# Input stage and attention in one block: no barrier between them, hand-placed SBUF, first operands loaded inside the input stage

## The reference

```python
def attn(x, w_attn, w_proj, adapter, gating):     # B=2, T=1024, C=512, 32 heads of 16
    q, k, v = split(x @ w_attn.T)                 # then rotary embedding on q and k
    attn = softmax(causal(q @ k.T / 4))
    y = attn @ v
    y = y + gating * softmax(q @ ak.T / sqrt(C)) @ av   # ak, av from 10 adapter rows
    return y @ w_proj.T

x = x + layernorm(attn(layernorm(x)))
x = x + layernorm(ffn(layernorm(x)))              # silu(x Wg.T) * (x Wu.T) @ Wd.T, F=1376
```

## Time and profile before

| | before |
|---|---|
| time, median of 3 runs | 1303.68 us (1301.52 to 1308.1) |
| the profiled execution's own time | 1300.54 us |
| span of the profile, first to last instruction | 1298.6 us |
| PE, DVE, ACT, POOL busy in the span | 88%, 56%, 39%, 21% |
| mean granted clock of PE | 0.928 |

### The profile page before, as it was taken

The page is one execution under the profiler, slowest core; times in us unless marked ns, Lnnn a source line. Parts: engine busy times, 40 slices in busy tenths (PEclk is TensorE's granted clock), DMA queues, the critical chain, the costliest instruction groups (busy, mean ns, idle before and its releaser), DMA issues. The chain is left out here.

```text
span 1298.6 us, 18975 instructions
## 1 busy us (share of the span) xinstructions
PE 1142.8 (88%) x7036; PEld 773.0 (60%) x7036; DVE 721.0 (56%) x968; ACT 507.5 (39%) x1058; POOL 269.3 (21%) x261
## 2 busy tenths in 40 slices
PE   3999998389999999999999994883999999999996
PEld 1777887145445444444444433662787787887785
DVE  4756755376777777777777513894223423324323
ACT  3133223025666666666666652441111111111111
POOL 1524524701111111111111111663000100001001
PEclk9999999558999999999999966886999999999998
DMA  7346346862444443434430005882100200200200
GB/s 259 97 112 171 112 115 180 160 105 50 77 84 89 85 77 76 75 75 75 76 75 19 18 25 177 254 284 81 65 1 1 97 1 2 98 1 17 81 1 33
DMA packets 82515, 113.01 MB, mean 87 GB/s; under 512 B 24964, under 2 KB 42500, under 8 KB 82436
## 3 DMA queue, kind: packets, MB, share of 16 engines
q1 hardware_dynamic: 82436, 111.92, 34.2%
HBM read 68.83 MB, written 42.21 MB: 86 GB/s over the span
## 5 line engine op out<-in xcount | busy, mean ns | idle before, releaser
L700 ACT ACTIVATE prob<-ps_s 128x512 f32<-128x512 f32 (+3 forms) x768 | 314.9, 505 | 190.1 <-PE ps_s L811 181.5
L723 DVE TENSOR_REDUCE neg<-ps_m 128x2 f32<-128x1024 f32 (+2 forms) x224 | 248.8, 1147 | 108.7 <-PE ps_m L781 73.8
L811 PE MATMUL ps_s<-q_op,k_op 50*128 50x512 f32 (+2 forms) x768 | 264.2, 449 | 29.0 <-ACT prob L700 26.0
L776 PE MATMUL ps_m<-k_op,q_op 48*128 48x512 f32 (+2 forms) x768 | 200.9, 428 | 34.4 <-DMA vg<-v_groups 23.0
L811 PEld LDWEIGHTS ps_s<-q_op,k_op 50*128 50x128 f32 x768 | 122.7, 192 | 158.7 <-ACT prob L700 93.8
L678 POOL TENSOR_SCALAR_AFFINE_SELECT prob<-prob 128x512 f32<-128x512 f32 x128 | 81.6, 637 | 445.1 <-ACT prob L700 445.1
L825 PE MATMUL ps_y<-prob,vg 128*17 128x512 f32 (+3 forms) x1536 | 155.6, 525 | 0.6 <-POOL prob L678 0.6
L1216 DVE TENSOR_TENSOR hf<-sl,ps_u 128x512 f32<-128x512 f32 (+1 forms) x44 | 30.2, 687 | 189.4 <-PE ps_u L72 189.4
L776 PEld LDWEIGHTS ps_m<-k_op,q_op 48*128 48x128 f32 x768 | 103.4, 199 | 51.4 <-issue 23.7
L723 DVE TENSOR_REDUCE neg_far<-ps_m 128x4 f32<-128x512 f32 (+2 forms) x96 | 97.6, 1045 | 37.9 <-PE ps_m L781 37.9
L1285 PE MATMUL ps_d<-w_ffn_high,wp_high 128*128 128x512 f32 (+1 forms) x352 | 115.6, 391 | 0.0
(11 more groups left out here) (161 smaller groups left out, 1769.2 us busy)
## 6 DMA issues: line engine op xcount, KB each, us to landing
raw<-in_w_ffn SPq DMA_DIRECT2D x16, 520.0 KB, 5.5
k_op<-k_parts SPq DMA_DIRECT2D x32, 256.0 KB, 5.1
q_op<-q_parts SPq DMA_DIRECT2D x64, 128.0 KB, 6.0
y_heads<-y_sb SPq DMA_DIRECT2D x32, 256.0 KB, 5.0
v_groups<-v_out SPq DMA_DIRECT2D x16, 272.0 KB, 3.9
vg<-v_groups SPq DMA_DIRECT2D x16, 272.0 KB, 6.9
x<-in_x SPq DMA_DIRECT2D x4, 1024.0 KB, 12.8
q_parts<-part_h SPq DMA_DIRECT2D x16, 256.0 KB, 2.9
```

Of the source, the lines that this page charges most:

```text
L700: act.activation(prob[:, v % NPROB, h, unit_cols(u)], ps_s[:, y % NS, unit_cols(u)], ACT.Exp, scale=D ** -0.5).then_inc(s_exp, 1)
L723: nc.vector.tensor_reduce(to[:, :, pairs[0]:pairs[-1] + 1, i - TT * c], scores, axis=AX.X, op=ALU.max, negate=True).then_inc(a_read, 1)
L776: last = nc.tensor.matmul(ps_m[:, g % 2, s, base:base + wide], q_op[buf][r, c, pair, (i - TT * c) * P:(i - TT * c + 1) * P], k_op[buf][r, ...
L811: nc.tensor.matmul(ps_s[:, y % NS, lo:BLK], k_op[buf][r, pair, j * P:(j + 1) * P], q_op[buf][r, c, pair, lo:BLK], start=True, stop=True)\
```

## The change

The two stages become one block. There is no barrier between them: each engine goes on from its last instruction of the input stage to its first of attention, and waits there only for the semaphores that guard the memory it takes over (`inputs_done`). SBUF is laid out by hand (`Map`): `k_op0`, `q_op0`, all `vg` and the masks have room of their own, the other three operand buffers lie over `x`, `wqk_h` and `wqk_l`. `x` has two buffers in place of four, so blocks 2 and 3 of x are loaded later. The loop over b is unrolled. Masks and the ones of `k_op0` are built by POOL before the first block, the ones of `k_op1` before block 3. ACT issues the loads of groups 0 and 1 itself, in blocks 2 and 3, right behind high_of(1). PE goes through 10 entries before the first unit in place of 27, and group 0's units carry the rest: after its four c = 0 units everything up to (0, "turn", 1) has been issued. `heads` and `wp_high` move before group 1, `wp_low` before group 2's first mask. `wp_raw` is loaded behind maxima(0, 1). The statistics and normalization that each block makes for the next are dropped in block 3, where they were not used.

```diff
+def load_group(engine, d, operands, op_in, n):
+    q_op, k_op, vg = operands
+    ...
+    for s in range(2):
+        r = 64 * s
+        engine.dma_start(k_op[buf][r:r + 2 * D].bitcast(F32), k[n, s]).then_inc(op_in[buf], 16)
+        engine.dma_start(k_op[buf][r + 2 * D:r + 3 * D].bitcast(F32), k[n, s, 0:D]).then_inc(op_in[buf], 16)
+        for c in range(HB):
+            engine.dma_start(q_op[buf][r + D:r + 3 * D, c].bitcast(F32), q[n, s, c]).then_inc(op_in[buf], 16)
+            engine.dma_start(q_op[buf][r:r + D, c].bitcast(F32), q[n, s, c, 0:D]).then_inc(op_in[buf], 16)
+    engine.dma_start(vg[buf][:], d["v_groups"][n]).then_inc(op_in[buf], 16)
...
         rstd_of(0)
+        build_masks(pool, passed, ident_h, causal_h, mask_const)
+        ones_below(pool, passed, k_op[0], op_const[0])
...
+                    if b == 1 and step == (high_of, 1):
+                        act.wait_ge(op_const[half], 2)
+                        for s in range(2):
+                            act.wait_ge(parts_out[s], 16 * 4 * 2 * HB)
+                            act.wait_ge(v_stored[s], 16 * 2 * HB)
+                        load_group(act, d, operands, op_in, half)
...
-    first_main = at[(1, EARLY)]
+    first_main = at[(0, "turn", 0)] + 1
...
-        if u == p == 0:
+        if p == 0 and u == 0 or n == p == 0 and u == TT:
             goal = at.get((n + 2, EARLY), len(order))
-            rate = sum(read_time(e) for e in order[todo:goal]) / sum(spot_time[i:i + NU * 2])
+            end = i + (NU - u) * 2
+            if n == u == 0:
+                goal, end = at[(0, "turn", 1)] + 1, i + TT * 2
+            rate = sum(read_time(e) for e in order[todo:goal]) / sum(spot_time[i:end])
...
+        maxima(0, 0)
+        load(2)
+        maxima(0, 1)
+        inputs_done(sp, "xn", "ya")
+        sp.dma_start(wp_raw[:], d["wp"]).then_inc(wp_in, 16)
...
+        pe.wait_ge(mask_in, 32)
+        inputs_done(pe, "rope")
         for g in range(first_main):
             for_maxima(g)
+        inputs_done(pe, "v_out", "pT", "ya_out")
```

More of the change, by code:

```diff
@@ L562, in stage_attention @@
             todo += 1
[L563 removed]
+        if i + 1 == end:
             beside[n, u, p] += range(todo, goal)
             todo = goal
[L567 to L850 removed]
@@ new lines, in _ @@
+    @block.gpsimd
+    def _(pool):
+        inputs_done(pool, "qk")
+        wait_alone(pool, passed, done["low"][0][1], done["low"][1])
+        for buf in range(2, NBUF):
+            ones_below(pool, passed, k_op[buf], op_const[buf])
+        inputs_done(pool, "parts")
+        for rows in (32, 64):
+            pool.memset(inv[rows:rows + 32], 0.0).then_inc(inv_const, 1)
+        wait_alone(pool, passed, inv_const, 2)
+        for n in range(NG):
+            if n == 2:
+                inputs_done(pool, "rot")
+                pool.wait_ge(wp_high, 1)
+                pool.tensor_tensor(wp_l[:], wp_raw[:], wp_h[:].bitcast(F32), op=ALU.subtract)
+            for u, (c, j) in enumerate(units):
+                if j < TT * c:
+                    continue
+                pool.wait_ge(s_exp, HG * (NU * n + u + 1))
+                diag = prob[:, (NU * n + u) % NPROB, :, (j - TT * c) * P:(j - TT * c + 1) * P]
+                pool.affine_select(out=diag, in_=diag, compare_op=ALU.is_ge, fill=0.0, base=0,
+                                   pattern=[[0, HG], [1, P]], channel_multiplier=-1).then_inc(masked, 1)
@@ new lines, in _, with take_y @@
+    @block.scalar
+    def _(act):
+        def take_y(n, c):
+            act.wait_ge(pv, NU * n + units.index((c, TT * (c + 1) - 1)) + 1)
+            if n:
+                act.wait_ge(y_out[c], 16 * n)
+            act.activation(y_sb[:, c], ps_y[:], ACT.Copy).then_inc(y_ready, 1)
+        inputs_done(act, "high", "low", "scores", "v")
+        for n in range(NG):
+            if n == 1:
+                inputs_done(act, "ya", "rot")
+                act.activation(heads[:].rearrange("p (h w) -> p h w", w=D), over(ident[0:KR, 0:H], D, 2), ACT.Copy)
+                act.wait_ge(wp_in, 16)
+                act.activation(wp_h[:], wp_raw[:], ACT.Copy).then_inc(wp_high, 1)
+            for u in range(NU):
+                v = NU * n + u
+                if v >= NPROB:
+                    act.wait_ge(pv, v - NPROB + 1)
+                for h in range(HG):
+                    y = HG * v + h
+                    act.wait_ge(s_ps, y + 1)
+                    act.activation(prob[:, v % NPROB, h, unit_cols(u)], ps_s[:, y % NS, unit_cols(u)], ACT.Exp,
+                                   scale=D ** -0.5).then_inc(s_exp, 1)
+                if u == 0 and n:
+                    take_y(n - 1, 1)
+                if u == TT:
+                    take_y(n, 0)
+        take_y(NG - 1, 1)
```

1242 lines of the change are left out of this document (617 added, 625 removed).

## The result

| | before | after |
|---|---|---|
| median | 1301.51 us (20 runs, 1289.35 to 1327.12) | 1305.34 us (20 runs, 1301.79 to 1313.72) |
| ratio after / before | | 1.0059, 95% interval 1.0032 to 1.0086 |
| the profiled execution: time, span, mean granted clock | 1300.54, 1298.6 us, 0.928 | 1311.89, 1310.2 us, 0.916 |

A forecast was written before the change was run, and what follows sets the result against it. It took the handoff's 22.98 us PE gap and the half-clock ramp as the loss; group 1's first scores 14.4 us earlier, less 3.0 later, gave 11.4 us net and 1292.3 us against the median 1303.68, range 1278 to 1303.

The forecast's parts named there:

- The gap: PE's idling at the handoff from input stage to attention: all 22.98 us were to go.
- C: Rival: in blocks 2 and 3 late stores and dearer ACT issues take most of the gain; 1300 us, chance 0.20.
- X: The time of group 1's first scores: forecast at 299.6 us, 14.4 us earlier than before.
- s: The end of the input stage's last adapter product on PE: 223.0 us before, forecast at 229.8.
- masks in the input stage: POOL's masks and ones run beside DVE's first normalization and delay the stage by 0.7 us.
- ACT's issues and the transfers, blocks 2 and 3: ACT's 13 issues delay PE 2.0 us a block, 4.1 in all; later-landing stores add 2 us.
- units with c = 0: Group 0's first units, carrying 15 entries where before 7, at DVE's price: 18 us.
- second row wait: Before group 0's first scores with c = 1, PE waits for the second turn's rows: 4.8 us.
- units with c = 1: Group 0's later units with 24 entries, the clock rising midway: 31 us, between 26 and 38.
- later costs: Behind group 1's first scores: heads and wp_high make PE wait 2.5 us, wp_low costs 0.5 us.
- D: Rival: in blocks 2 and 3 ACT waits for stores behind the loads, 12 us a block; 1314 us, chance 0.10.
- rival B: Behind the handoff PE's clock stays up or returns at once; net gain 17.4, 1286 us, chance 0.20.

The follow-up runs named there:

- e3: e1 plus 13 DMAs of 16 bytes a row, into a tile nobody reads, issued by ACT behind high_of(1); ratio to before 1.0036.
- e1: Changed kernel with the loads issued by SP at the start of blocks 2 and 3, none by ACT; ratio to before 0.9962.
- e2: Changed kernel with ACT's loads moved to the start of blocks 2 and 3, ahead of high_of(0); ratio to before 0.9884.
- e6: e5 with both groups' loads issued by SP behind its last stores, still without the barrier; ratio to before 1.0103.
- e4: Changed kernel with attention's list of entries as in the kernel before, loads still on ACT behind high_of(1); ratio to before 0.9996.
- e5: Changed kernel with the edits of e2 and e4 together; 1286.65 us, ratio to before 0.9894.
- e10: Changed kernel with wp_raw loaded ahead of the first rows, and heads and wp_high ahead of the first exponential; ratio to before 1.0006.
- e11: e9 with a needless 1.9 us copy on ACT at the start of the sixth group; ratio to before 0.9948.
- e7: e5 with a matmul that nobody reads behind entries of the ramp, about 20 of them; ratio to before 0.9989.
- e9: e5 with wp_raw loaded ahead of the first rows, and heads and wp_high ahead of the first exponential; 1281.1 us, ratio to before 0.9853.
- e8: Changed kernel with ACT's loads one step later, behind exp_of(0); ratio to before 1.0126.

## Why the prediction was wrong

The gap went as forecast, and so did the kind of the waits. Their sizes didn't, and no rival described the result: C came nearest in number (1300), but by a mechanism that didn't occur. X was read from the row at 314.02. The same row now stands at 308.69, where 299.6 was forecast. (By counting, the group's first scores stand 0.65 us ahead of that row, in both kernels.) The terms (s was forecast as 229.8 and is 234.8):

| term | forecast | measured |
|---|---|---|
| masks in the input stage | +0.7 | -1.1 (end of block 1) |
| ACT's issues and the transfers, blocks 2 and 3 | 4.1 + 2 | 12.8 |
| s to group 0's first scores (11.5 + 4.5) | 16.0 | 14.8 |
| units with c = 0 | 18 | 19.2 |
| second row wait | 4.8 | 4.7 |
| units with c = 1 | 31 | 35.2 |
| second group longer than before ("later costs") | 3.0 | 7.9 |

1. **ACT's 13 issues: the step that failed.** I took 13 issues at 0.47 us, 6.1 us in all, the exponential 2.0 us late by it, and carried that 2.0 through to PE. The issues took 8.3, which my upper price of 0.64 us had (8.3 us exactly). But what was queued behind them wasn't only late: it fell onto the start of POOL's `part_l`, and `a_prob` grew from 0.49 to 2.51 us. In the order of before it began 1.2 us ahead of `part_l` and was through. I had named the steps behind the issues and priced them as if they slid without changing. So the 2.0 us a block were mis-sized in two steps: the exponential was 4.5 us late in place of 2.0, and the delay grew by another 2.0 on its way to PE. e3 shows that issues without bytes suffice for most of it, even where they took 6.3 us; e1 and e2 show that without issues at that place most of the loss is gone. What is left of the 12.8 is the share of the unrolled stage and the transfers: e6, with no load in the stage, takes 1.5 us more than before for blocks 2 and 3, and kernels with early loads at the block's start 0 to 3.5 on top. The Trainium skill (SBUF — State Buffer, SBUF: two separate sides) says that a VectorE operation with two SBUF inputs and a GpSimd one that reads SBUF take the shared port pair in turn, and the one that starts second is fully blocked. By that rule `a_prob`, begun at 158.16, ends only after `part_l` (160.33); the trace agrees, it ended at 160.67.
2. **The transfers: rivals C and D fell.** Stores in blocks 2 and 3 landed in 3.1 to 5.3 us in the median of each kind (before, in block 2, 2.9 to 4.0, the `v_out` stores 4.0), not in 8 to 14, and e3 loses most of it without bytes. The trace agrees with the rule of the Trainium skill that the prediction quotes (transfers of all issuing engines interleave): SP's stores landed in these times beside ACT's loads. The same section of the Trainium skill calls the issue time usually small relative to the DMA. Here an issue took 0.31 to 1.44 us and its load landed after 5.0 to 7.2. That is small, and no comfort: on ACT, among steps that PE waits for, it was most of the cost.
3. **The ramp: the forecast was near, the comparison missing.** The row waits were sized about right (5.43 and 4.74 against 4.5 and 4.8). What I never asked was what the handoff would give with the old list, under which 17 entries cover the wait. e4 and e5 show it: 7 to 8 us better (e4 against after, e5 against e2). So of the 10.2 us of the two row waits the earlier units earned back only some 3. The units with c = 1 were mis-sized as well: 35.2 us and not 31, near the 38 of a half clock throughout. The clock was at half for 20 of these 35 us.
4. **Later costs and the clock.** I priced `heads` and `wp_high` at their own 2.5 us. The wait came (2.15 us), but from it on the clock was at half for 20 of 24 us, and the group took 7.9 us more than before to the mark of group 2. This is a second step that failed: the wait was priced at its own length. e10, that one edit, gives 9.5 us in that group; e11 makes the same loss again at a place of my choosing. Against rival B the clock did fall, as forecast, in the ramp. The prediction quotes the Trainium skill for the rule that activity releases the slow clock. e7 agrees with it: at 0.50 in 225:235, with the additions 1.00 from 235 us on. A PE busy for 9.85 of 10 us at 0.50 (e5, 265 to 275 us) remains, as the earlier trace rows, a stretch where the slow clock is not released at once.

Added up at group 3 (after less before, 2.6 us): the gap gives 23.0; blocks 2 and 3 take 12.8, less 1.1 from block 1; the row waits take 10.2 and the second group 7.9 more. These make +6.8; the rest of group 0's entries and units, which ran partly at full clock, give 4.2 back. The forecast was a gain of 11.4, so it missed by 14.0. Up to rounding these are 6.7 in blocks 2 and 3, 4.9 in the later costs, 4.2 in the units with c = 1, 1.2 in those with c = 0, less 1.8 in the term of the masks and 1.3 up to group 0's first scores and in the second row wait.

**What stays open.** Why the clock falls in some groups of some executions with no wait over 0.32 us in sight (after's 540 to 557, e9's 305 to 315). In after, e1, e5 and e8 such a fall begins some 7 us behind a group's first scores and costs 10 us in two groups; the same stretch passes without a fall in most other groups. Why block 1 ends 1.1 us earlier. And whether `a_prob` alone could have been saved, by another order on POOL, wasn't tried.

## What to carry to other kernels

DMA issues on a compute engine are instructions of that engine: put them where its next consumer has slack, which the trace shows as its idle time, and check what each delayed step will newly run beside. A wait on the critical engine must be priced with the clock that it may lose; 2 us cost 8 to 10 here, so work that holds a feeding engine belongs where that engine is idle, not where it is merely free on average. When a change removes a gap and reorders the work behind it, cost the two apart: the old order behind the new handoff was the better half.

## What the runs showed of the hardware

- An issue of the same 13 loads on ACT took 0.31 to 0.45 us each where little else ran (e2), and up to 1.32 and 1.44 us beside SP's stores (after, blocks 2 and 3); with tiny transfers at the same place up to 0.58 and 1.74 (e3, blocks 2 and 3).
- A DVE operation of 0.49 us took 2.51 us when it began 0.2 us behind a POOL addition of 2.36 us.
- One wait of PE of 1.65 to 2.16 us was followed by 20 to 24 us at half clock within 24 us (after, e4, e11), with PE busy for 9.3 to 10 of 10 us in most of that time; in e11 the stretch was steady until then.
